# Selective state space input: order of the projections, the normalisations and the taps

## The reference

```python
# sublayer 0: D = 256 channels, K = 4 taps, all to the left
h = x * rsqrt(mean(x * x) + EPS) * rms_w
proj = h @ in_W + in_b
x1, g = proj[..., :D], proj[..., D:]
x1 = silu(depthwise_conv(x1, conv_w, padding=(K - 1, 0)) + conv_b)
# ... scan over x1 gives y ...
out = (silu(g) * y) @ out_W + out_b + residual
# sublayer 12: 128 channels, 3 taps (one left, one right), no rms step
x1 = silu(depthwise_conv3_same(u @ Win + b_in))
out = scan(x1) * silu(u @ Wg + bg) @ Wout + bout
```

## Time and profile before

| | |
|---|---|
| median of three runs | 5654.21 us (5651.17 to 5657.56) |
| the profiled execution, its own time | 5634.33 us |
| its span, first to last instruction | 5632.3 us |
| mean granted TensorE clock | 0.927 of 2.4 GHz |
| input stage of sublayer 0 | 37.60 us to 101.62 us of the span |
| input stage of sublayer 12 | 4131.12 us to 4158.82 us |

### The profile page before, as it was taken

How to read it: one execution, slowest core, us unless ns; L and a number is a source line. 1 busy time by engine, 2 the same in 40 slices (tenths; PEclk the granted TensorE clock), 3 DMA queues, 4 the chain that set the end, 5 groups by cost and what they waited for, 6 DMA issues and landing times. The chain is left out here.

```text
span 5632.3 us, 90553 instructions
## 1 busy us (share of the span) xinstructions
PE 4704.7 (84%) x33501; PEld 2071.8 (37%) x33596; DVE 3785.4 (67%) x4596; ACT 3148.3 (56%) x5990; POOL 1686.2 (30%) x1468
## 2 busy tenths in 40 slices
PE   6677678997789977899778998499867899799999
PEld 2233234443333344333443333266323344333344
DVE  6899668886689834899348982777549600799400
ACT  6655445766458843588435885344465422488621
POOL 0666316885122225222351220000016300223100
PEclk8899889998889979899888999699979999799999
DMA  0000011110111134111341110000000000111100
GB/s 28 0 0 0 4 59 32 45 43 25 31 65 48 53 111 142 63 49 53 122 144 44 52 48 15 6 6 2 4 10 0 21 0 2 43 38 36 41 0 15
DMA packets 120302, 211.62 MB, mean 38 GB/s; under 512 B 34982, under 2 KB 71442, under 8 KB 118484
## 3 DMA queue, kind: packets, MB, share of 16 engines
q1 hardware_dynamic: 110580, 182.00, 10.5%
q10 hardware_dynamic: 4320, 15.73, 0.9%
q0 software_dynamic: 4992, 8.41, 0.6%
HBM read 153.93 MB, written 52.00 MB: 37 GB/s over the span
## 5 line engine op out<-in xcount | busy, mean ns | idle before, releaser
L999 ACT ACTIVATE l_core_probs<-l_core_ps_scores_b 128x512 f32<-128x512 f32 (+3 forms) x3840 | 1609.6, 508 | 582.4 <-PE l_core_ps_scores_b L907 418.0
L1101 DVE TENSOR_REDUCE l_core_chunk_max<-l_core_ps_scores_a 128x2 f32<-128x1024 f32 (+3 forms) x1280 | 1253.6, 1021 | 83.5 <-PE l_core_ps_scores_a L892 47.9
L907 PE MATMUL l_core_ps_scores_b<-l_q_rows_sb,l_k_rows_sb 64*128 64x512 bf16 (+3 forms) x3840 | 947.6, 332 | 39.0 <-ACT l_core_probs L999 16.5
L892 PE MATMUL l_core_ps_scores_a<-l_k_rows_sb,l_q_rows_sb 64*128 64x512 bf16 (+3 forms) x3840 | 740.4, 345 | 104.3 <-DVE l_core_chunk_max L1101 45.2
L1050 POOL TENSOR_SCALAR_AFFINE_SELECT l_core_probs<-l_core_probs 128x512 f32<-128x512 f32 x512 | 325.5, 636 | 1171.5 <-ACT l_core_probs L999 1166.6
L922 PE MATMUL l_core_ps_acc<-l_core_probs,l_v 128*9 128x512 f32 (+3 forms) x6144 | 648.0, 494 | 15.8 <-ACT l_core_out_sums L973 8.9
L907 PEld LDWEIGHTS l_core_ps_scores_b<-l_q_rows_sb,l_k_rows_sb 64*128 64x128 bf16 x3840 | 304.7, 94 | 699.7 <-ACT l_core_probs L999 612.4
L1101 DVE TENSOR_REDUCE l_core_neg_max<-l_core_ps_scores_a 128x2 f32<-128x256 f32 (+3 forms) x640 | 493.6, 820 | 93.5 <-PE l_core_ps_scores_a L852 92.2
L2009 POOL TENSOR_TENSOR l_scan_bx<-l_xs,l_scan_b_rows 128x1024 f32<-128x1024 f32 x192 | 452.3, 2356 | 224.8 <-DVE l_scan_states L2019 216.8
L2019 DVE TENSOR_TENSOR_SCAN l_scan_states<-l_scan_ps_decay,l_scan_bx 128x1024 f32<-128x1024 f32 x192 | 439.8, 2290 | 40.4 <-POOL l_scan_bx L2009 15.0
L1020 POOL TENSOR_TENSOR l_core_probs_decayed<-l_core_probs,l_decay 128x1536 f32<-128x1536 f32 (+2 forms) x160 | 394.0, 2487 | 146.7 <-ACT l_core_probs L999 146.7
(11 more groups left out here) (323 smaller groups left out, 7525.7 us busy)
## 6 DMA issues: line engine op xcount, KB each, us to landing
l_slots_weights<-m_both_dram SPq DMA_DIRECT2D x78, 512.0 KB, 4.7
l_q_rows_sb<-l_q_rows SPq DMA_DIRECT2D x128, 96.0 KB
l_k_rows_sb<-l_k_rows SPq DMA_DIRECT2D x128, 96.0 KB
l_heads_out<-l_core_out_sums SPq DMA_DIRECT2D x300, 32.0 KB
l_q_rows<-l_proj_parts SPq DMA_DIRECT2D x36, 256.0 KB, 2.4
l_k_rows<-l_proj_parts SPq DMA_DIRECT2D x36, 256.0 KB, 3.2
l_q_rows_sb<-l_q_rows SPq DMA_DIRECT2D x128, 64.0 KB
l_k_rows_sb<-l_k_rows SPq DMA_DIRECT2D x128, 64.0 KB
```

Of the source, the lines that this page charges most:

```text
L892: mm = nc.tensor.matmul(slot[:, i, 0:w], qs[n % 3][rows, p, qt * P:(qt + 1) * P], ks[n % 3][rows, p, c * NT:c * NT + w], start=True, stop= ...
L907: mm = nc.tensor.matmul(pb[m % 3][:, 0:w], ks[n % 3][rows, p, kt * P:(kt + 1) * P], qs[n % 3][rows, p, q0:q0 + w], start=True, stop=not diag)
L999: nc.scalar.activation(pt[:, ts % RP, j, 0:w], pb[m % 3][:, 0:w], ACT.Exp, scale=scale).then_inc(b_free, 1)
L1101: nc.vector.tensor_reduce(to, pa[e % 2][:, :, 0:width_a(qt, c)], AX.X, ALU.max, negate=True).then_inc(a_free, 1)
```

## The change

Only `ssm_input` changes. TensorE now does, for each batch, the channels of both tiles and then the gates of both tiles. Channels use banks 0 and 1, gates banks 2 and 3, each with semaphores of their own. ScalarE takes in the same order, channels of both tiles, gates of both tiles, then the Silu of the batch before. VectorE takes tap after tap, and within a tap the halves in turns. Two of the next batch's normalisations stand between the rows of taps: tile 2b + 2 after tap 0, tile 2b + 3 after tap 1. Tap 0 waits for the channels only, the last tap waits for the Silu of the batch before. All loops are written out. The running sum and the output have buffers of their own (`half`, `cv`). The lines removed are those printed above; the diff shows what takes their place.

```diff
@@ ssm_input
-        cv = sb("conv", [P, 2, 2, S])
+        half = sb("conv_part", [P, H, S])
+        cv = sb("conv", [P, H, S])
...
+        RT = 2 // H
+        ends = taps - 1 - left
...
+                def channels(t):
+                    if rms:
+                        pe.wait_ge(h_ready, t + 1)
+                    for m in range(H):
+                        if t >= RT:
+                            pe.wait_ge(c_free, H * (t - RT) + m + 1)
+                        nc.tensor.matmul(pp[:, t % RT * H + m, :], win[:, m * P:(m + 1) * P],
+                                         hh[:, t % 2, :] if rms else xn[:, t * NT:(t + 1) * NT],
+                                         start=True, stop=True).then_inc(c_ready, 1)
...
+                for b in range(B):
+                    channels(2 * b)
+                    channels(2 * b + 1)
+                    gates(2 * b)
+                    gates(2 * b + 1)
...
-                act.wait_ge(chain, 1)
-                act.sem_inc(p_free, 4)
+                act.wait_ge(pads, 2 if ends else 1)
                 nc.scalar.preload_act_table_set("silu_and_others")
...
+                for b in range(B):
+                    take(2 * b)
+                    take(2 * b + 1)
+                    take_gates(2 * b)
+                    take_gates(2 * b + 1)
+                    if b:
+                        silu(b - 1)
                 silu(B - 1)
...
+                def normed(t):
+                    tok = slice(t * NT, (t + 1) * NT)
+                    if t >= 2:
+                        dve.wait_ge(g_ready, H * (t - 1))
+                    nc.vector.scalar_tensor_tensor(hh[:, t % 2, :], xn[:, tok], rmsw[:, 0:1], fac[:, tok],
+                                                   ALU.mult, ALU.mult).then_inc(h_ready, 1)
 
                 def convolve(b):
-                    for h in range(H):
-
-                        dve.wait_ge(p_free, 4 + (2 * b + 2) * M)
-                        dve.wait_ge(xs_done, H * b + h + 1)
-                        for k in range(taps):
...
+                    dve.wait_ge(pads, 2 if ends else 1)
+                    for k in range(taps):
+                        for h in range(H):
+                            n = b * (taps - 1) * H + k * H + h
+                            xin = xp[:, h, b, k:k + S]
+                            dst = cv[:, h, :] if k == taps - 1 else half[:, h, :]
                             if k == 0:
+                                dve.wait_ge(c_free, H * (2 * b + 1) + h + 1)
+                                if b:
+                                    dve.wait_ge(conv, H * (b - 1) + h + 1)
+                                a = nc.vector.tensor_scalar(dst, xin, cvw[:, h, 0:1], cvb[:, h:h + 1], ALU.mult, ALU.add)
                             else:
+                                dve.wait_ge(chain, n - H + 1)
+                                if k == taps - 1 and b:
+                                    dve.wait_ge(xs_done, H * (b - 1) + h + 1)
+                                a = nc.vector.scalar_tensor_tensor(dst, xin, cvw[:, h, k:k + 1], half[:, h, :],
                                                                    ALU.mult, ALU.add)
+                            a.then_inc(conv if k == taps - 1 else chain, 1)
+                        if rms and k < 2 and b < B - 1:
+                            normed(2 * b + 2 + k)
 
                 if rms:
                     normed(0)
+                    normed(1)
+                for b in range(B):
                     convolve(b)
```

More of the change, by code:

```diff
@@ L1658, in ssm_input @@
         hh = sb("rms_normed", [P, 2, NT])
[L1659 removed]
+        half = sb("conv_part", [P, H, S])
+        cv = sb("conv", [P, H, S])
         pp = ps("proj", [P, 4, NT])
[L1661 to L1663 removed]
+        h_ready, c_ready, c_free, g_ready, g_free, conv, xs_done, chain, pads = (sem(n) for n in (
+            "h", "channels", "channels_free", "gates", "gates_free", "conv", "xs", "chain", "pads"))
+        RT = 2 // H
+        ends = taps - 1 - left
         with nc.Block() as block:
@@ new lines, in gates @@
+                def gates(t):
+                    for m in range(H):
+                        if t >= RT:
+                            pe.wait_ge(g_free, H * (t - RT) + m + 1)
+                        nc.tensor.matmul(pp[:, 2 + t % RT * H + m, :], win[:, (H + m) * P:(H + m + 1) * P],
+                                         hh[:, t % 2, :] if rms else xn[:, t * NT:(t + 1) * NT],
+                                         start=True, stop=True).then_inc(g_ready, 1)
+                for b in range(B):
[3 more added lines that the diff above has]
+                    gates(2 * b + 1)
@@ L1679, in _, with take @@
             @block.scalar
             def _(act):
-                act.wait_ge(chain, 1)
-                act.sem_inc(p_free, 4)
+                act.wait_ge(pads, 2 if ends else 1)
                 nc.scalar.preload_act_table_set("silu_and_others")
[L1685 to L1697, removed]
+                def take(t):
+                    b, at = t // 2, left + t % 2 * NT
+                    for m in range(H):
+                        act.wait_ge(c_ready, H * t + m + 1)
+                        nc.scalar.activation(xp[:, m, b, at:at + NT], pp[:, t % RT * H + m, :], ACT.Identity,
+                                             bias=bin_[:, m:m + 1]).then_inc(c_free, 1)
@@ L1699, in silu, with take_gates @@
+                def take_gates(t):
+                    for m in range(H):
+                        act.wait_ge(g_ready, H * t + m + 1)
+                        nc.scalar.activation(gate[:, m, t * NT:(t + 1) * NT], pp[:, 2 + t % RT * H + m, :], ACT.Silu,
+                                             bias=bin_[:, H + m:H + m + 1]).then_inc(g_free, 1)
                 def silu(b):
@@ L1701, in silu @@
                         act.wait_ge(conv, H * b + h + 1)
[L1702 to L1707, removed]
+                        nc.scalar.activation(xs[:, h, b * S:(b + 1) * S], cv[:, h, :], ACT.Silu).then_inc(xs_done, 1)
+                for b in range(B):
[5 more added lines that the diff above has]
+                        silu(b - 1)
                 silu(B - 1)
@@ L1712, in _ @@
                 nc.vector.memset(xp[:, :, :, 0:left], 0.0).then_inc(pads, 1)
-                if taps - 1 - left:
+                if ends:
                     nc.vector.memset(xp[:, :, :, left + S:PADDED], 0.0).then_inc(pads, 1)
[L1715 to L1725, removed]
-                                                       ALU.mult, ALU.mult).then_inc(h_ready, 1)
```

22 lines of the change are left out of this document (removed).

## The result

The changed kernel took 5624.5 us (median of five runs, 5622.4 to 5633.8) beside 5655.4 us for the kernel before (median of five, the three of the table and two more). The ratio is 0.9954 with a 95% interval of 0.9943 to 0.9966: 26 us less, between 19 and 32 (the medians alone are 30.8 apart). Forecast were 22.8 us less and 5631.4, with a range of 5623 to 5642. The direction and the size held, and the range did by 1.5 us at its lower end.

A forecast was written before the change was run, and what follows sets the result against it. Two input stages, 91.7 us together, were taken as bound by waits, no engine full. Gains of 16.3 us (sublayer 0) and 6.5 (sublayer 12) make 22.8, so the median 5654.2 becomes 5631.4 us; range 5623 to 5642.

The forecast's parts named there:

- The start of sublayer 0: Sublayer 0's input stage: tap 0 of half 0 starts at 44.69 in place of 51.09, 6.4 us earlier.
- The steps of the taps: VectorE, sublayer 0: a row of taps independent of the row just before takes 1.195 us, against 1.32 when dependent.
- The lower bound: Sublayer 0's row-of-taps step lies between 1.195 and 1.32 us; the prediction took 1.195 as nearest.
- The later batches: Sublayer 0, batches 1 and 2: 9.93 us each on VectorE; batch 3, without normalisation, 8.61 us.
- both waits of 3.19 us: Sublayer 0's loop: VectorE's two waits before a batch's second normalisation, 3.19 us each, count towards the gain.
- Sublayer 12: Its input stage: tap 0 at 4135.2 in place of 4138.63, end at 4151.5 for 4158.13; gain 6.6 us, taken as 6.5.
- the wait in batch 1: Sublayer 12: VectorE, free at 4138.7, waits 0.7 us for the sixth product, done at 4139.4.
- The sum: Both input stages: 16.3 us from sublayer 0 plus 6.5 from sublayer 12, 22.8 us less in all.
- its three terms: Forecast's own bounds: clock's rise 2 x 1.7 us, placed waits 1 us, runs 3.3 us to either side.
- Rows without overlap: Rival, sublayer 0: rows of taps wait for the previous row's end despite turns; 4.9 us more, 5636.3 us; chance 0.16.
- The low clock: Rival, both input stages: TensorE stays at 1.2 GHz, 1.70 us per product; 2.2 us slower, 5656.4 us; chance 0.03.
- The gain that doesn't show: Rival, later stages: shifted starts and clock give back half the gain, 5642.8 us; chance 0.13.

The follow-up runs named there:

- the second trace: The changed kernel run once more, unedited, on chip 1: 5594.9 us beside 5624.2 for the kernel before, ratio 0.9949.
- the two experiments that undo them: Changed kernel with gates behind the channels of their own tile, 5644.0 us; changed kernel with both normalisations ahead of the taps, 5640.9 us.
- the halves apart: Changed kernel with the taps of one half after those of the other: 5601.3 us, on the chip where the changed kernel took 5594.9.

## Why the prediction was right

**The start of sublayer 0.** Right in kind, larger in size. The channels of both tiles are the first four products, and tap 0 follows the third. Forecast was 7.1 us into the stage (44.69 - 37.60); measured were 5.96 and, in the second trace, 7.13. The difference is the clock's rise, 3.8 and 6.9 us into the stage, which the prediction had allowed 1.7 us for. Of the earlier first tap the order of the products carries 1.9 us (8.99 - 7.13, gates with their tile), and the place of the normalisations is worth 2.6 us of the stage, by the two experiments that undo them.

**The steps of the taps.** Right: 1.19 measured, 1.195 taken. The lower bound was the right choice, and the halves apart gave back 3.05 us where 3.0 were worked out. The Trainium skill, VectorE: DVE Perf Modes, "The DRAIN you can't avoid", says that the semaphore between operations costs nothing. For two rows of 128x1024 of which the second waits for the first these traces say 0.13 us, the distance of 1.32 to 1.19. The same section of the Trainium skill adds that a next operation that is not held starts earlier. The early starts of the turns agree with that; the prediction had left this out where it said that the rule has no room for them.

**The later batches.** Right, in size and in kind: 9.96 us against 9.93, and no wait of VectorE. That both waits of 3.19 us would go was read from the code, and the trace bears it out, though no run undoes it alone. From the normalisation of tile 2 (46.13) to the last Silu's end (84.33) it was 38.2 us; from 46.52 to 84.67 the prediction had 38.15.

**Sublayer 12.** The mechanism was right, two terms were off. The gain is 5.8 us where 6.5 were taken. The first term is the start: TensorE was to start 0.45 ahead of VectorE's clearing and 0.88 earlier than before. It starts 0.04 ahead of it (4129.09 to 4129.13), 0.47 earlier with respect to VectorE. The next stage's row, from which I took the distance, was no measure for this one. The second is the wait in batch 1, 0.90 for 0.7. In the second trace the gain is 7.1, since the clock rose earlier.

**The sum.** 22.8 forecast, 23.0 and 22.9 in the two traces' stages. That it fits to 0.2 us is partly luck: sublayer 0 gave 17.2 and 15.8 where 16.3 were worked out, sublayer 12 gave 5.8 and 7.1 where 6.5 were, and the two misses cancel in both traces. The medians say 30.8 and 29.3, and both intervals hold 23. By the ratios it is 26 and 29 us, so the excess is 3 to 8 us, and it is not settled; the prediction had no term for it. It took the median to 5624.5, 1.5 us above the range's lower end and outside the 5625 to 5638 that the prediction gave as the forecast's own bounds (its three terms add up to 7.7 us either way, so 5624 to 5639 would have been the sum). That the range held there is luck too. Up to 3 us of the excess lie in one attention stage, and kernels without the new order show them as well. Whether the rest is of the same kind would take many more runs of kernels that differ only in a delay: 17 runs of the kernel before on one chip already lie 14 us apart.

**The rivals.** Rows without overlap: out. The low clock: its price was right, it didn't come, as TensorE stays at 1.00 with 68% busy and idle times up to 1.29 us. The gain that doesn't show: two first traces of before and after lie only 11.7 us apart in span (5632.3 and 5620.6), and it would have looked so, had the medians of one chip not been there. The profiled execution of before had the short form of two stages that are 12 us longer each on chips 5 and 7. That accounts for the 20 us between that execution and the median, which the prediction could not place; as the chip of that execution is not on record, it is the likely cause and not a shown one.

## What to carry to other kernels

Where stages end in a barrier and no engine is full, find the first instruction of the engine that will be the bound, list what it truly needs, and make exactly that first: here four products and not eight. A chain of rows of 128x1024 that each read the one before lost about 0.13 us per link on VectorE here, and two chains in turns won it back. Compare stages, not spans: the length of the stages that the change touches was good to 1.4 us each, while spans of single traces moved by 24 us in two stages of another kind.

## What was not expected of the hardware

- The stage of sublayer 5 that streams the experts' weights took 174 to 178 us on chip 1 and 189 to 195 us on chips 5 and 7, with a DMA share of 0.56 and 0.50 in the rows above. Sublayer 7's twin took 174 to 179 and 187 to 195. Together that is 22 to 39 us between the traces of different chips.
- Clearings of 128x1024 that wait for each other come 1.19 us apart though each lasts 0.91: 0.28 us between the end of one and the start of the next, where dependent rows of taps leave 0.04.

```profile
83.60 0.91 DVE L1770 MEMSET l_in_idle<- 128x1024 f32 x1 [0.16 <-issue]
84.79 0.91 DVE L1770 MEMSET l_in_idle<- 128x1024 f32 x1 [0.28 <-DVE l_in_idle L1770]
```

- The clock of TensorE rose 3.0 us after the first product in one trace of the changed kernel and 6.1 us after it in the other, with the same queue ahead of it. That moved the stage by 1.4 us.
